# Conditional residual product: tiles 2 and 3 transposed on VectorE, banks of the head exchanged, identity adds on GpSimd

## The reference

```python
u = jax.nn.gelu(encoded_utterance @ W_proj + b_proj, approximate=False)
W_u, W_e = (weight_matrix[:D], weight_matrix[D:])
logits = (u @ W_u)[:, None, :] + jnp.einsum('bnd,dc->bnc', element_embeddings, W_e)
...
x = x + _L0_cond_ref(cond_1024, x, ...)
```

## Time and profile before

| | us |
|---|---|
| median of 3 runs | 346.98 (346.65 to 347.87) |
| the profiled execution, its own time | 347.7 |
| its span | 345.4 |
| TensorE busy | 339.6 (98%) |
| VectorE busy | 261.7 (76%) |
| GpSimd busy | 277.2 (80%) |
| ScalarE busy | 247.0 (72%) |

### The profile page before, as it was taken

The page is one execution under the profiler, slowest core; times in us unless marked ns, Lnnn a source line. Parts: engine busy times, 40 slices in busy tenths (PEclk is TensorE's granted clock), DMA queues, the critical chain, the costliest instruction groups (busy, mean ns, idle before and its releaser), DMA issues.

```text
span 345.4 us, 7856 instructions
## 1 busy us (share of the span) xinstructions
PE 339.6 (98%) x2706; PEld 328.7 (95%) x2706; DVE 261.7 (76%) x301; ACT 247.0 (72%) x424; POOL 277.2 (80%) x196
## 2 busy tenths in 40 slices
PE   7999999999999999999999999999999999999996
PEld 3758999999999999999999999999999999999996
DVE  2869977788777778877777897777789777778811
ACT  3646877877777787777778777777877777787741
POOL 0357998888989888898988889898888989888860
PEclk9999999999999999999999999999999999999999
DMA  7998697888799788879978887997887799788116
GB/s 257 331 180 236 123 238 201 221 194 204 176 228 241 195 219 196 198 180 229 237 200 218 195 197 178 232 233 202 219 197 197 175 235 237 197 209 210 83 56 228
DMA packets 72264, 70.64 MB, mean 205 GB/s; under 512 B 2880, under 2 KB 67392, under 8 KB 68032
## 3 DMA queue, kind: packets, MB, share of 16 engines
q1 hardware_dynamic: 72256, 70.53, 80.5%
HBM read 36.96 MB, written 33.55 MB: 204 GB/s over the span
## 4 chain that ended last, share of the span: by engine, by line
PE 89%; DVE 1%; ACT 0%; issue 0%
PE banks L743 30%; PE banks L747 29%; PE banks L745 29%; DVE work L509 1%; DVE banks L509 0%; DVE banks L552 0%; ACT snap_rows L461 0%; ACT y L504 0%; ACT hi L399 0%
## 5 line engine op out<-in xcount | busy, mean ns | idle before, releaser
L743 PE MATMUL banks<-t_hi,hi 128*128 128x256 f32 x496 | 140.5, 283 | 0.2 <-ACT snap_rows L461 0.2
L745 PE MATMUL banks<-t_lo,hi 128*128 128x256 f32 x496 | 140.4, 283 | 0.0
L747 PE MATMUL banks<-t_hi,lo 128*128 128x256 f32 x496 | 140.4, 283 | 0.0
L743 PE MATMUL banks<-w_hi,hi 128*128 128x256 f32 x372 | 105.3, 283 | 0.4 <-ACT banks L424 0.4
L745 PE MATMUL banks<-w_lo,hi 128*128 128x256 f32 x372 | 105.3, 283 | 0.0
L747 PE MATMUL banks<-w_hi,lo 128*128 128x256 f32 x372 | 105.3, 283 | 0.0
L509 DVE STREAM_TRANSPOSE work<-quad_raw 128x1024 f32<-128x1024 f32 (+1 forms) x62 | 100.7, 1624 | 3.6 <-DMA quad_raw<-in_x 3.6
L743 PEld LDWEIGHTS banks<-t_hi,hi 128*128 128x128 f32 x496 | 95.2, 192 | 0.6 <-issue 0.6
L747 PEld LDWEIGHTS banks<-t_hi,lo 128*128 128x128 f32 x496 | 95.2, 192 | 0.0
L745 PEld LDWEIGHTS banks<-t_lo,hi 128*128 128x128 f32 x496 | 95.2, 192 | 0.0
L316 POOL TENSOR_TENSOR lo<-work,hi 128x1024 fp32r<-128x1024 f32 x31 | 74.8, 2413 | 21.7 <-ACT hi L391 21.7
(11 more groups left out here) (71 smaller groups left out, 401.7 us busy)
## 6 DMA issues: line engine op xcount, KB each, us to landing
out<-y SPq DMA_DIRECT2D x31, 1024.0 KB, 4.5
quad_raw<-in_x SPq DMA_DIRECT2D x120, 256.0 KB, 5.7
head_raw<-in_x SPq DMA_DIRECT2D x2, 512.0 KB, 5.7
w_e<-in_L_cond_weight_matrix SPq DMA_DIRECT2D x2, 512.0 KB, 6.2
w_proj_sb<-in_L_cond_W_proj SPq DMA_DIRECT2D x1, 1024.0 KB, 10.0
w_u<-in_L_cond_weight_matrix SPq DMA_DIRECT2D x1, 1024.0 KB, 12.3
quad_raw<-in_x SPq DMA_DIRECT2D x8, 128.0 KB, 9.5
out<-y SPq DMA_DIRECT2D x3, 256.0 KB, 2.1
```

The lines of the kernel that those rows point to most:

```text
L743: pe.matmul(psum[:, t, :], a_hi[:, 2 * j + t, :], b_hi[:, j, :], start=False, stop=False, skip_group_check=True)
L745: pe.matmul(psum[:, t, :], a_hi[:, 2 * j + t, :], b_lo[:, j, :], start=False, stop=False, skip_group_check=True)
L747: last = pe.matmul(psum[:, t, :], a_lo[:, 2 * j + t, :], b_hi[:, j, :], start=False, stop=(j == T - 1), skip_group_check=True)
```

## The change

- Tiles 2 and 3 are loaded in the pattern of the quads, by four transfers behind W_proj, and turned by VectorE into the same banks into which TensorE turned them (`turn_second`). TensorE's eight transposes of them go.
- GpSimd adds the identity to slices 1 to 3 of `w_e`; slice 0 stays on VectorE.
- h goes to bank 7 and the flips of cond and h to bank 6, which they exchange. Quad 0 (and every even quad) sums A in bank 7 and C in bank 6, before 6 and 1. The first seed of A is copied from `bias_psum` itself by ScalarE, ahead of the copy of the bias into SBUF on VectorE, which waits for it. The first seed of C no longer waits for an evacuation.
- In the head TensorE takes the hi by hi product of slice j+1 ahead of the lo by hi product of slice j. ScalarE turns its order round: cond, the four roundings of `t_sum`, then tiles 2 and 3. VectorE makes S3 ahead of S2, and S1's low part behind the bias. One filler matmul more.

```diff
-WARM_UP = 6
+WARM_UP = 7
...
-        direct = head_raw[:, :].rearrange("p (n d) -> p n d", n=HEAD)
+        direct = head_raw[:, 0:T * TILE].rearrange("p (n d) -> p n d", n=T)
+        second = head_raw[:, T * TILE:HEAD * TILE].rearrange("p (m n w) -> p m n w", m=NM, n=T)
...
-        flip_psum = banks[3][:, 1, :].rearrange("p (j b) -> p j b", j=NJ)
-        h_psum = banks[3][:, 0, :]
+        flip_psum = banks[3][:, 0, :].rearrange("p (j b) -> p j b", j=NJ)
+        h_psum = banks[3][:, 1, :]
...
-        a_bank = [bank(6).rearrange("p (t c) -> p t c", t=T), bank(2).rearrange("p (t c) -> p t c", t=T)]
-        c_bank = [bank(1).rearrange("p (t c) -> p t c", t=T), bank(3).rearrange("p (t c) -> p t c", t=T)]
+        a_bank = [bank(7).rearrange("p (t c) -> p t c", t=T), bank(2).rearrange("p (t c) -> p t c", t=T)]
+        c_bank = [bank(6).rearrange("p (t c) -> p t c", t=T), bank(3).rearrange("p (t c) -> p t c", t=T)]
...
-            load_direct(1)
             sp.dma_start(cond_sb[:, :], cond).then_inc(cond_loaded, 16)
             sp.dma_start(w_proj_sb[:, :, :], w_proj_dram).then_inc(w_proj_loaded, 16)
+            for q in range(NQ):
+                sp.dma_start(second[Q * q:Q * (q + 1)], x_dram[q, :, :, T:HEAD, :]).then_inc(second_loaded, 16)
...
+            pool.wait_ge(ident_ready, 1)
+            for j in range(1, NJ):
+                pool.wait_ge(w_e_loaded[j // 2], 16)
+                diag = diagonal(j)
+                pool.tensor_tensor(diag, diag, ident[:, :], ALU.add).then_inc(w_diag_ready, 1)
...
-            hi_t(0)
-            act.wait_ge(cond_flipped, 1)
-            act.copy(cond_t[:, :, :], flip_psum).then_inc(cond_ready, 1)
-            for n in range(1, 4):
+            for n in range(4):
                 hi_t(n)
+            for n in range(T, HEAD):
+                direct_hi(n)
...
+                elif p == 0:
+
+                    act.wait_ge(h_ready, 1)
+                    act.wait_ge(bias_summed, 1)
+                    source = bias_psum
...
+                act.copy(a_bank[p], source[:, left].unsqueeze(1).to_broadcast([P, T, H])).then_inc(a_seeded, 1)
...
+            def turn_second(t):
+                transpose(direct_psum[t].rearrange("p j (i m) -> p m j i", m=NM),
+                          second[:, :, t, :].rearrange("p m (k j) -> p m j k", k=Q)).then_inc(second_turned, 1)
...
+            dve.wait_ge(second_loaded, LOADS)
+            dve.wait_ge(direct_lo_ready, T)
+            for t in range(T):
+                turn_second(t)
             for n in range(T, HEAD):
                 split_direct(n)
             turn_up(0, 0, True)
             turn_low(0, 0, True)
             sum_s1(0, 0, True)
+            sum_s3(0, 0, True)
             sum_s2(0, 0)
-            split_s1(0, 0)
-            sum_s3(0, 0, True)
-            dve.wait_ge(bias_summed, 1)
+
+            dve.wait_ge(a_seeded, 1)
             dve.tensor_copy(bias[:, :], bias_psum).then_inc(bias_copied, 1)
             dve.wait_ge(bias_copied, 1)
             dve.tensor_tensor(bias_step[:, :], bias_psum[:, right], bias[:, left], ALU.subtract).then_inc(bias_ready, 1)
+            split_s1(0, 0)
```

More of the change, by code:

```diff
@@ L142, in build_cond_residual @@
         w_e_loaded = [sem(f"w_e_loaded{n}") for n in range(2)]
-        direct_loaded = [sem(f"direct_loaded{c}") for c in range(HEAD_CHUNKS)]
+        direct_loaded = sem("direct_loaded")
+        second_loaded = sem("second_loaded")
         direct_flipped = sem("direct_flipped")
+        second_turned = sem("second_turned")
         direct_hi_ready = sem("direct_hi_ready")
@@ L162, in build_cond_residual @@
         w_diag_ready = sem("w_diag_ready")
+        first_diag_ready = sem("first_diag_ready")
         w_hi_ready = [sem(f"w_hi_ready{j}") for j in range(NJ)]
@@ L222, in first_half, with diagonal @@
             return quad_raw[0][:, n * T * TILE:(n + 1) * T * TILE].rearrange("p (m n w) -> p m n w", m=NM, n=T)
+        def diagonal(j):
+            return w_e[:, j, :].rearrange("p (a r) -> p a r", r=NJ)[:, :, j]
         def stores_before(k, p):
@@ L238, in load_quad @@
                                  x_dram[q, :, :, bass.ds(HEAD + k * QUAD, QUAD), :]).then_inc(quad_loaded[p], 16)
-            def load_direct(c):
-                sp.dma_start(direct[:, c * T:(c + 1) * T, :],
-                             x[:, c * T:(c + 1) * T, :]).then_inc(direct_loaded[c], 16)
             def load_w_e(n):
                 sp.dma_start(w_e[:, 2 * n:2 * n + 2, :], w_e_dram[:, 2 * n:2 * n + 2, :]).then_inc(w_e_loaded[n], 16)
-            load_direct(0)
+            sp.dma_start(direct, x[:, 0:T, :]).then_inc(direct_loaded, 16)
             for n in range(2):
                 load_w_e(n)
-            load_direct(1)
             sp.dma_start(cond_sb[:, :], cond).then_inc(cond_loaded, 16)
             sp.dma_start(w_proj_sb[:, :, :], w_proj_dram).then_inc(w_proj_loaded, 16)
+            for q in range(NQ):
+                sp.dma_start(second[Q * q:Q * (q + 1)], x_dram[q, :, :, T:HEAD, :]).then_inc(second_loaded, 16)
             sp.dma_start(b_proj_sb[:, :], b_proj_dram).then_inc(b_proj_loaded, 16)
@@ L356, in direct_hi @@
             def direct_hi(n):
-                act.wait_ge(direct_flipped, n + 1)
+                if n < T:
+                    act.wait_ge(direct_flipped, n + 1)
+                else:
+                    act.wait_ge(second_turned, n - T + 1)
                 act.copy(x_hi[n // T][:, n % T, :, :], direct_psum[n % T]).then_inc(direct_hi_ready, 1)
@@ L362, in _ @@
             for j in range(1, NJ):
-                act.wait_ge(w_diag_ready, j + 1)
+                act.wait_ge(w_diag_ready, j)
                 act.copy(w_hi[:, j, :], w_e[:, j, :]).then_inc(w_hi_ready[j], 1)
-            for n in range(T, HEAD):
-                direct_hi(n)
+            act.wait_ge(cond_flipped, 1)
+            act.copy(cond_t[:, :, :], flip_psum).then_inc(cond_ready, 1)
             def hi_t(n):
@@ L416, in seed_a, with seed_c @@
             def seed_a(k, p, first):
+                source = bias
+                if not first:
+                    act.wait_ge(c21_out, k - 1)
+                elif p == 0:
+                    act.wait_ge(h_ready, 1)
+                    act.wait_ge(bias_summed, 1)
+                    source = bias_psum
+                else:
+                    act.wait_ge(bias_ready, 1)
+                    act.wait_ge(evacuated, HEAD_CHUNKS)
+                act.copy(a_bank[p], source[:, left].unsqueeze(1).to_broadcast([P, T, H])).then_inc(a_seeded, 1)
+            def seed_c(k, p, first):
                 if first:
@@ L421, in seed_a @@
                         act.wait_ge(evacuated, HEAD_CHUNKS)
[L422 to L429, removed]
                 else:
@@ L473, in _ @@
             hi_a22(0, 0, True)
+            seed_a(0, 0, True)
             hi_s2(0, 0, True)
+            seed_c(0, 0, True)
             hi_s3(0, 0, True)
-            seed_a(0, 0, True)
-            seed_c(0, 0, True)
             hi_s4(0, 0, True)
@@ L605, in _ @@
             dve.wait_ge(ident_ready, 1)
-            add_identity(0)
-            dve.wait_ge(w_diag_ready, 1)
+            dve.wait_ge(w_e_loaded[0], 16)
+            first_diag = diagonal(0)
+            dve.tensor_tensor(first_diag, first_diag, ident[:, :], ALU.add).then_inc(first_diag_ready, 1)
+            dve.wait_ge(first_diag_ready, 1)
             dve.tensor_copy(w_hi[:, 0, :], w_e[:, 0, :]).then_inc(w_hi_ready[0], 1)
             split_direct(0)
-            add_identity(1)
             split_direct(1)
-            add_identity(2)
-            add_identity(3)
             for j in range(NJ):
@@ L618, in _ @@
             b11, b12, b21, b22 = b_of[:, 0, 0], b_of[:, 0, 1], b_of[:, 1, 0], b_of[:, 1, 1]
-            dve.wait_ge(w_diag_ready, NJ)
+            dve.wait_ge(w_diag_ready, NJ - 1)
             dve.tensor_tensor(t_sum[:, 0, :, :], b12, b11, ALU.subtract).then_inc(t_summed, 1)
@@ L682, in _ @@
             for t in range(T):
-                pe.wait_ge(direct_loaded[0], 16)
+                pe.wait_ge(direct_loaded, 16)
                 flip(direct_psum[t], by_j(direct[:, t, :]), direct_flipped)
@@ L688, in product, with high @@
                 return pe.matmul(banks[0][:, t, :], a[:, t, j, :], b[:, j, :], start=first, stop=last)
+            def high(j):
+                pe.wait_ge(w_hi_ready[j], 1)
+                for t in range(T):
+                    if j == 0:
+                        pe.wait_ge(direct_hi_ready, t + 1)
+                    product(t, x_hi[0], w_hi, j, first=(j == 0))
+            high(0)
             for j in range(NJ + 1):
+                if j + 1 < NJ:
+                    high(j + 1)
                 if j < NJ:
[L692 to L696, removed]
                     for t in range(T):
@@ L700, in _ @@
                         product(t, x_lo[0], w_hi, j)
[L701 to L704, removed]
                 if j == NJ - 1:
```

## The result

The changed kernel takes 347.62 us (median of 20 runs, 347.11 to 349.0) against 346.81 (20 runs, 346.44 to 348.24): ratio 1.0021, 95% interval 1.0013 to 1.003. That is +0.8 us, and +0.9 when both were run once more (347.67 against 346.78; ratio 1.0031, 1.0013 to 1.005).

A forecast was written before the change was run, and what follows sets the result against it. VectorE's chain from quad 0's landing to quad 1's transposes was taken to bound the kernel. Later landing +1.03 us, chain -0.19, TensorE's savings nothing: +0.84, giving 347.8 us on the median's scale, range 346.3 to 349.0.

The forecast's parts named there:

- The loads: Tiles 2 and 3 in 512 B pieces ahead of quad 0 in SP's queue delay its landing by 1.03 us.
- The rival of two slow starts: Each switch from plain to strided loads starts at 159 GB/s: landing slips 1.98 us, time 348.8; chance 0.27.
- the slow stretch of 159 GB/s: DMA rate at 14 to 16 us in the trace before, the first 2 us after the switch to quad loads.
- The chain behind the landing: VectorE from quad 0's lower transposes to quad 1's takes 8.61 us against 8.80 before.
- T+8.61: Forecast start of quad 1's transposes on VectorE; T is the start of quad 0's lower transposes.
- What set the kernel before: VectorE's reaching quad 1's transposes decides; they start 8.80 us behind the landing of quad 0's second half.
- the slow first stretch: The very first strided loads, tiles 2 and 3, were taken at 3.30 us of 2.35 to 3.30, landing at 15.1.
- TensorE's savings are hidden: In the head, the eight transposes dropped (0.87 us) and waits removed from TensorE win nothing in the total.
- What TensorE does earlier is free: TensorE's work in the head, ahead of quad 0's M7, costs nothing as long as it is not late.
- A wait of about 1 us inside quad 0: TensorE enters quad 0 0.1 us earlier, meets a chain 0.84 us late, and waits mostly ahead of M6 and M7.
- The reorder: VectorE's S3 ahead of S2 fills a 0.65 us gap; the seed wait gives 0.4 back, so 0.19 us is won.
- The profile's own time: Time around the span in the profiled execution before: 2.3 us, 347.7 with a span of 345.4.

The follow-up runs named there:

- before_again: The unchanged kernel before, run and profiled once more: 346.85 us, ratio 1.0002 to the kernel before.
- after_again: The unchanged changed kernel, run and profiled once more: 347.67 us, ratio 1.0031 to the kernel before.
- extra_transposes: The changed kernel with eight more 128 x 128 transposes on TensorE into a bank nobody reads: 347.71 us, ratio 1.0036 to the kernel before.
- flips_back: The changed kernel with tiles 2 and 3 again loaded plainly and turned by TensorE's eight transposes, other parts kept: 347.16 us, ratio 1.0005 to the kernel before.

## Why the prediction was right, and where not

The forecast was +0.84 us, the measurement +0.8 to +0.9. The agreement is partly luck: the chain in the head gave only half of it (+0.4 us of span), and 0.46 us outside the span, which the forecast had not seen, made up the rest.

- **The loads.** Right in kind, and near in size as far as can be told: 1.03 forecast, 0.8 from the mean landings against the kernels with the old queue, 1.5 against the one profile with the plain load. Its 0.85 us of time are no measure of the slip, since its bias copy waited 1.25 us for TensorE. The rival of two slow starts falls: the slow stretch of 159 GB/s is not tied to a switch of pattern. In before_again the same switch moved 218. The changed kernel's switches lie elsewhere, as w_u runs at 14 to 16 us (312 GB/s): the strided tiles come at 10 to 12 us, with 260 GB/s in the first profile and 193 and 227 in the two microseconds of after_again, and quad 0 has the queue from 16 us on, with 220 and 190 in its first microsecond. None of them has two at 159. The same stretches of the changed kernel as in the earlier trace rows:

```profile
5.00:13.00 8.00, 8.00 (x39) 6.26 (x38) 6.52 (x12) 2.94 (x5) 1.68 (x3) 1.00 1.08 346
14.00:16.00 2.00, 2.00 (x7) 1.04 (x6) 1.72 (x2) 2.00 (x5) 1.46 (x2) 1.00 1.02 312
16.00:21.00 5.00, 4.82 (x19) 3.05 (x19) 3.40 (x3) 2.53 (x8) 3.53 (x3) 1.00 1.22 223
```

- **The chain behind the landing.** T+8.61 forecast, T+8.54 to T+8.64 measured; S3 in the gap, the wait of 0.32 for the seed (forecast 0.4), M7 6.2 us behind quad 1: all as put.
- **What set the kernel before.** This step failed. "The start of quad 1's transposes is the landing of quad 0's second half plus 8.80 us" holds in the one profile with a late landing. In before_again, whose time is that of the median, TensorE's head releases the second evacuation and quad 1 starts at 29.89, not 30.52. The changed kernel's chain therefore costs the difference to 29.89, and not to 30.52. The spans' medians moved by 0.4 us, not 0.84.
- **Tiles 2 and 3.** Forecast to land at 15.1 with TensorE 1.0 us late for them. They landed by 13.5 and 14.1, and TensorE waited 0.2. The term that was wrong is the slow first stretch that I took for them. It was without effect on the sum.
- **TensorE's savings are hidden.** Right for the changed kernel, shown by extra_transposes. "What TensorE does earlier is free" is not right for the kernel before, where TensorE's head decides in an execution of median time: with the plain load the spans' median is 344.5, against 344.9 before and 344.9 with the transposes back on TensorE. So the strided load costs 0.8 to 0.9 us of span and what TensorE saves gives 0.4 back. "A wait of about 1 us inside quad 0" was 0.7 in one profile and 1.5 in the other.
- **The reorder.** 0.19 forecast, 0.1 to 0.2 in the rows, not seen in the times.
- **The profile's own time.** Taking 2.3 us around the span for both kernels was wrong. It is 1.86 before and 2.32 after, and these 0.46 us are half of the loss.

What of the change brings the 0.46 us stays open. All kernels built on the changed one have it (2.26 to 2.38), and both others don't (1.84 to 1.86). It is therefore not the strided load, the transposes on VectorE, the order of S3 or the snapshots. Left are GpSimd's adds, the banks and the seed, TensorE's order in the head, what flips_back kept of ScalarE's, the seventh filler, and two more semaphores. None of them was tried by itself.

## What to carry to other kernels

When two chains end within half a microsecond of each other, one profile can show only the one that was late in that execution, as that of the earlier trace rows did: take a second profile before saying which wait decides, and look how far the profiled run is from the median. Compare spans and times separately, since a change can cost time outside the span. A wait for an instruction that was itself ready, but queued behind one that waits for a later stage, can be taken away by order alone: here two moved snapshots brought 1.7 us of span against the changed kernel, while the change itself had moved the span by 0.4.

## What was not expected of the hardware

Time less span goes with the program (1.8 to 1.9 us in all but two runs of the kernel before, 2.1 to 2.5 after; the two had 2.2 and 2.3), and its median moved by 0.46 us between two kernels whose first and last instructions are alike. The landing of the same loads scatters by 1.65 us (20.07 to 21.72 with the queue of before), in which one execution moved only 159 GB/s in two microseconds where another moved 218. GpSimd's add to a diagonal of 128 x 128, of which no row existed, took 0.67 us the first time, and two took 1.01:

```profile
6.46 0.67 POOL L315 TENSOR_TENSOR w_e<-w_e,ident 128x128 f32<-128x128 f32 x1 [4.97 <-DMA w_e<-in_L_cond_weight_matrix]
7.70 1.01 POOL L315 TENSOR_TENSOR w_e<-w_e,ident 128x128 f32<-128x128 f32 x2 [0.57 <-DMA w_e<-in_L_cond_weight_matrix]
```
